# Two norm reductions of a two-layer transformer kernel: one loop over both sources in place of one loop after the other

## The reference

```python
x = L0_attn_x                                   # (8, 2048, 1024) float32
# layer 0
xn = layernorm(x)
s = causal_attention_16_heads(xn, Wq, bq, Wk, bk, Wv, bv, Wo, bo)   # with rope
g = silu(ffn_int8(xn, w_gate, w_up, w_down))
x = x + s * g
# layer 1
xn = layernorm(x)
q = xn @ Wq + bq;  k = xn @ Wk + bk;  v = xn @ Wv + bv
q_sq = sum(q * q, axis=-1)
k_sq = sum(k * k, axis=-1)
dist_sq = q_sq[:, :, None] + k_sq[:, None, :] - 2.0 * (q @ k.T)
scores = exp(-dist_sq)
attn = softmax(scores, axis=-1)
s = (attn @ v) @ Wo + bo
g = silu(mix_of_8_adapters(xn))
x = x + s * g
```

## Time and profile before

| what | us |
|---|---|
| median of 2 runs | 3301.47 |
| the two runs | 3224.66 and 3378.28 |
| profiled execution, its own time | 3231.18 |
| its span on the slowest core (core 6), first to last instruction | 3229.6 |
| spans of the other seven cores | 3203.3 to 3225.4 |
| mean granted TensorE clock of the cores | 0.776 to 0.781 |

### The profile page before, as it was taken

How to read it: one execution, slowest core, us unless ns; L and a number is a source line. 1 busy time by engine, 2 the same in 40 slices (tenths; PEclk the granted TensorE clock), 3 DMA queues, 4 the chain that set the end, 5 groups by cost and what they waited for, 6 DMA issues and landing times.

```text
span 3229.6 us, 39546 instructions; the slowest of 8 cores (3203.3 to 3229.6 us)
## 1 busy us (share of the span) xinstructions
PE 2296.0 (71%) x15153; PEld 1262.9 (39%) x15302; DVE 878.0 (27%) x1693; ACT 861.8 (27%) x1189; POOL 80.4 (2%) x152
## 2 busy tenths in 40 slices
PE   2499989984666646796777777166787564887777
PEld 0244444431333213464664665043575221333333
DVE  1544444442232264433222112500110000122122
ACT  2111111112111145464444444111100223222222
POOL 0000001100000000000000000000000000000000
PEclk9699999997888865656556555588888895988888
DMA  4222222202101020101001000432143102011010
GB/s 120 30 30 30 30 30 34 36 7 52 20 14 19 1 52 1 60 2 60 2 1 60 2 2 11 170 94 72 59 133 97 26 0 52 1 52 39 14 52 27
DMA packets 58442, 128.65 MB, mean 40 GB/s; under 512 B 7561, under 2 KB 15755, under 8 KB 55700
## 3 DMA queue, kind: packets, MB, share of 16 engines
q1 hardware_dynamic: 33364, 90.46, 8.3%
q0 software_dynamic: 24896, 35.66, 7.3%
HBM read 142.88 MB, written 18.88 MB: 50 GB/s over the span
## 4 chain that ended last, share of the span: by engine, by line
PE 57%; ACT 16%; DVE 13%; issue 7%; DMA 5%; DVEq 1%; ACTq 0%; SPq 0%; POOL 0%; PEldq 0%; POOLq 0%
PE PS L886 8%; ACT EB L908 6%; PE PS L720 6%; PE PS L1192 5%; PE PS L592 5%; PE PS L601 5%; PE PS L1335 4%; PE PS L1164 4%; PE PS L1404 4%; PE PS L635 4%; PE PS L1275 2%; DVE PS L891 2%; ACT PRJ L728 2%; DVE ACC L646 1%; PE PS L952 1%
## 5 line engine op out<-in xcount | busy, mean ns | idle before, releaser
L886 PE MATMUL PS<-Q,K 64*128 64x128 bf16 x2176 | 274.1, 304 | 123.8 <-ACT EB L908 118.8
L908 ACT ACTIVATE EB<-PS,negBh 128x1152 bf16<-128x1152 f32 (+7 forms) x128 | 204.1, 1594 | 256.0 <-DVE PS L891 242.0
L886 PEld LDWEIGHTS PS<-Q,K 64*128 64x128 bf16 x2176 | 211.5, 135 | 152.9 <-issue 142.2
L1192 PE MATMUL PS<-XN,W1FULL 128*128 128x512 bf16 x747 | 177.4, 397 | 65.4 <-ACT Q L1207 18.7
L635 PE MATMUL PS<-HT,WDT 128*128 128x512 bf16 x745 | 191.3, 393 | 39.1 <-DVE HT L618 21.9
L720 PE MATMUL PS<-XN,WBLK 128*128 128x512 bf16 x746 | 205.0, 438 | 12.7 <-DVE K L735 5.1
L1164 PE MATMUL PS<-identw,PLAND 128*128 128x128 f32 x1024 | 142.6, 308 | 98.9 <-DMA PLAND<-Wsel 67.6
L891 DVE TENSOR_TENSOR PS<-PS,trinegT 128x128 f32<-128x128 f32 x256 | 76.7, 300 | 439.0 <-PE PS L886 430.7
L1164 PEld LDWEIGHTS PS<-identw,PLAND 128*128 128x128 f32 x1024 | 139.3, 223 | 104.1 <-issue 104.1
L592 PE MATMUL PS<-XN,WGT 128*128 128x512 bf16 x752 | 171.0, 383 | 8.5 <-DVE ACC L646 5.7
L601 PE MATMUL PS<-XN,WUT 128*128 128x512 bf16 x752 | 168.8, 379 | 0.8
(11 more groups left out here) (160 smaller groups left out, 2522.4 us busy)
## 6 DMA issues: line engine op xcount, KB each, us to landing
PLAND<-Wsel SPq DMA_DIRECT2D x64, 512.0 KB, 4.2
XF<-xT SPq DMA_DIRECT2D x1, 8192.0 KB, 35.8
XT<-xT SPq DMA_DIRECT2D x4, 2048.0 KB, 8.5
x1park<-XT SPq DMA_DIRECT2D x32, 256.0 KB
X1CH<-x1park SPq DMA_DIRECT2D x8, 1024.0 KB, 8.5
XT<-x1park SPq DMA_DIRECT2D x4, 2048.0 KB, 8.2
outT<-XT SPq DMA_DIRECT2D x32, 256.0 KB
LAND<-wg POOLq DMA_DIRECT2D x16, 256.0 KB, 4.6
```

The lines of the kernel that those rows point to most:

```text
L886: tS = P.op("tensor", lambda t, h=h, gi=gi, tt=tt, off=off: t.matmul(PS[:, off + tt * 128:off + (tt + 1) * 128], head_k(h, ts(tt, 128)), h ...
L908: s.activation(EB2[:, slot, 0:klen], PS[:, 0:klen], AF.Exp, bias=negBh[:, h:h + 1]), inc=True)
L1192: P.op("tensor", lambda t, fc=fc, j=j, n=n: t.matmul(BK(n), W1FULL[:, j, ts(fc, 128)], src_xn[:, j, ts(n, 512)], start=(j == 0), stop=(j = ...
```

## The change

The two passes over K and Q become one loop over c. In it ScalarE squares the chunk of K into slot c % 2 of `EB2`, VectorE squares the chunk of Q (as Q times Q) into slot c % 2 of `ETB`, seen as 128 x 2 x 2048, and TensorE does four matmuls for K into banks 0 to 3 and then four for Q into banks 4 to 7. Each square waits for the matmuls that read its slot two chunks earlier. The eight row copies on VectorE all stand after the loop.

```diff
-    tM = None
-    for src_, which in ((K, "k"), (Q, "q")):
-        tSq = None
-        for c in range(EC):
-            P.wait("scalar", tM)
-            tSq = P.op("scalar", lambda s, c=c, src_=src_: s.activation(
-                EB2[:, 0, :], src_[:, c, :], AF.Square), inc=True)
-            P.wait("tensor", tSq)
-            for n in range(4):
-                tM = P.op("tensor", lambda t, c=c, n=n: t.matmul(
-                    BK(n), negones[:, :], EB2[:, 0, ts(n, 512)],
-                    start=(c == 0), stop=(c == EC - 1)), inc=(n == 3))
-        P.wait("vector", tM)
-        dst_row = NKSQ_ROW if which == "k" else NQSQ_ROW
-        sclr = 1.0 if which == "k" else 0.25
-        tRw = None
+    tMsl = {0: None, 1: None}
+    tMq = {0: None, 1: None}
+    ETBf = ETB.rearrange("p s a b -> p s (a b)")
+    tMk = tMqq = None
+    for c in range(EC):
+        sl = c % 2
+        P.wait("scalar", tMsl[sl])
+        tks = P.op("scalar", lambda s, c=c, sl=sl: s.activation(
+            EB2[:, sl, :], K[:, c, :], AF.Square), inc=True)
+        P.wait("vector", tMq[sl])
+        tqs = P.op("vector", lambda v, c=c, sl=sl: v.tensor_mul(
+            ETBf[:, sl, :], Q[:, c, :], Q[:, c, :]), inc=True)
+        P.wait("tensor", tks)
         for n in range(4):
-            tRw = P.op("vector", lambda v, n=n, dst_row=dst_row, sclr=sclr:
-                       v.tensor_scalar_mul(dst_row[0:1, ts(n, 512)],
-                                           BK(n)[0:1, :], sclr), inc=(n == 3))
-        P.wait("tensor", tRw)
-        P.wait("scalar", tRw)
+            tMk = P.op("tensor", lambda t, c=c, n=n, sl=sl: t.matmul(
+                BK(n), negones[:, :], EB2[:, sl, ts(n, 512)],
+                start=(c == 0), stop=(c == EC - 1)), inc=(n == 3))
+        tMsl[sl] = tMk
+        P.wait("tensor", tqs)
+        for n in range(4):
+            tMqq = P.op("tensor", lambda t, c=c, n=n, sl=sl: t.matmul(
+                BK(4 + n), negones[:, :], ETBf[:, sl, ts(n, 512)],
+                start=(c == 0), stop=(c == EC - 1)), inc=(n == 3))
+        tMq[sl] = tMqq
+    P.wait("vector", tMk)
+    P.wait("vector", tMqq)
+    tRw = None
+    for n in range(4):
+        tRw = P.op("vector", lambda v, n=n: v.tensor_scalar_mul(
+            NKSQ_ROW[0:1, ts(n, 512)], BK(n)[0:1, :], 1.0), inc=(n == 3))
+    tRw2 = None
+    for n in range(4):
+        tRw2 = P.op("vector", lambda v, n=n: v.tensor_scalar_mul(
+            NQSQ_ROW[0:1, ts(n, 512)], BK(4 + n)[0:1, :], 0.25),
+            inc=(n == 3))
+    P.wait("tensor", tRw2)
+    P.wait("scalar", tRw2)
     P.barrier()
```

## The result

Timed beside the kernel before, the changed kernel has a median of 3221.34 us (17 runs, 3183.85 to 3402.49) against 3261.25 (16 runs, 3224.66 to 3378.28). The ratio is 0.9878, with a 95% interval of 0.9831 to 0.9925: some 1.2% faster, within the 2% that I called the same. Runs in which half of the cores as a whole were slower at a lower clock are left out of this ratio; others with a few cores at a clock near 0.77, the profiled one among them, stay in, and the medians lie so far above the lowest times for both reasons. In a later set of runs the same kernel took 3183.63 to 3186.45 us in four runs beside a median of 3227.76 for the kernel before, ratio 0.9847 (0.9791 to 0.9902).

What follows compares the result with a forecast made beforehand. No engine full; in the norm stage ScalarE and TensorE alternate on one buffer. Q's squares off the chain 15.3 us, TensorE's clock some 11, the rest overlap: 46 us. 3231.2 - 46 = 3185 us, range 3168 to 3262.

Steps and rivals of the forecast that it cites:

- The chain: Norm stage: square and four matmuls alternate strictly on one buffer, 4.01 us a chunk, 70.3 us for the stage.
- ScalarE's squares: New loop: squares 1.86 us apart set the pace; third and fourth start late, the fourth by over 1 us.
- VectorE's product: New loop: each bf16 product of Q taken at 1.23 us; 2.29 as the other end costs 2 us of the gain.
- The clock in the loop: New loop: TensorE begins at the lower level, and the clock rises 3.9 to 5.9 us after the first matmul.
- the clock stays low: Rival, norm loop: clock stays at 0.5, gain 35 us, time 3196; chance 0.17 together with a swinging clock.
- Squares and products in each other's way: Rival, norm loop: ScalarE and VectorE slow each other to 3.1 us a chunk, gain 37, time 3194; chance 0.05.
- The step that failed: Head of last stage: TensorE's pause grows from 3.5 to 5.9 us, costed at nothing, up to 1 us.
- The lottery of the last stage: Last stage: a shifted start deals its granted clocks anew; four query groups some 6 us to either side.
- The level: Whole kernel: 46 us subtracted from the profiled execution's 3231.2 us, giving 3185, not from the timed runs' median.
- the likeliest case: Whole kernel: the forecast of 3185 us with the product at either price, own range 3174 to 3195; chance 0.68.
- A sign of being wrong: Last stage: query groups that take over 130 us each would show the forecast wrong.
- The slower rival: Rival, last stage: a lower clock, from 0.87 to 0.78, uses up the 46 us; chance 0.03.

Runs made afterwards that it cites:

- the two-slot kernel: Kernel before with both slots of EB2 used in turn and nothing else: stage 38.2 to 38.4 us, both stages 533.6 to 544.9 us.
- the kernels with one slot: Changed kernel with one slot for K's squares and one for Q's: stage 32.9 us, both stages 535.2 to 538.1 us.
- with ScalarE alone: Changed kernel with Q's squares moved from VectorE to ScalarE: stage 35.8 to 36.0 us, both stages 536.9 to 538.4 us.
- the kernel with K's norms in the Q projection: Changed kernel without the barrier, K's squares and matmuls moved into the Q projection, Q's squares split between VectorE and ScalarE: ratio to before 0.9808.
- the changed kernel's second profile: The changed kernel run once more, unaltered: stage 23.4 to 23.5 us, last stage 506.5 to 506.9 us, ratio to before 0.9847.
- the run with the fill: Changed kernel plus twelve unread matmuls between K's row copies and the barrier: stage 23.7 to 24.2 us, both stages 523.2 to 524.0 us on five cores.

## Why the prediction was right, and where it wasn't

The forecast was 3185 us, no change clear of 2%. The time of the stage came out by the mechanism that I gave; that the total did so too is in part luck. Point by point:

- **The chain.** That ScalarE and TensorE alternate for want of a second buffer, and that this bounds the stage, is shown by the two-slot kernel: 70.3 to 38.4 us by that alone.
- **ScalarE's squares.** I took 1.86 us from start to start; five in a row took 9.12 us, which is (9.12 - 1.90)/4 = 1.80. The third and fourth squares were held up as laid out (0.30 and 0.56 us, where I had 0.3 and over 1).
- **VectorE's product.** I took 1.23 from a row of another operation, and it measured 1.225; the other end, 2.29, is out. The Trainium skill, "VectorE: DVE Perf Modes", section "The perf-mode tier table", had given 1224 ns, and the trace agrees.
- **The clock in the loop.** I had it rise 3.9 to 5.9 us after the first matmul; it rose after 3.2. The 3.9 was a misreading: 2729.4 is where my window ended, and its mean of 0.59 over 4.0 us puts the rise near 3.3. Together with the squares this makes the stage 23.5 us instead of 24.5, and the gain 46.8 instead of 46. The rival "the clock stays low" had 0.17 and fell: this loop and those of the kernels with one slot and with ScalarE alone kept the higher level once they had it, with pauses of 1.3 us (one slot) and 0.8 us or less (ScalarE alone) between their bursts; the two-slot kernel lost it only in the pause between K and Q. For this loop the rule of the Trainium skill on small pauses between groups ("TensorE: Matmul & The Clock Gate", section "A second HAM failure mode: psum-queue depth-cycling") was not borne out by the trace.
- **Squares and products in each other's way.** They aren't: beside each other a square takes 1.90 us, as before, and a product 1.225, as in the kernel with K's norms in the Q projection, where ScalarE makes no squares beside it (1.23).
- **The step that failed** is "It started that stage at the lower level anyway [...], so I cost this at nothing, with up to 1 us". The pause ahead of the last stage grew from 3.5 to 5.9 us, as I had it, but the clock fell in it and stayed down for 12 us of work: 5.7 us, with the long head on 14 of 16 cores. The term was mis-sized by 5 us. With the pause filled the loss is gone (the last stage takes 499.3 to 500.0 us), so there is none without the pause. But the longer pause isn't the whole cause: with one slot each, with ScalarE alone and on two cores of the changed kernel itself the pause was as long, and the low head took 2.8 to 3.6 us, for which "nothing" would have been right. What made it long here stays open.
- **The lottery of the last stage.** I gave it 6 us to either side. Within the changed kernel's second profile the eight cores agree within 0.4 us, but the two-slot kernel, with the same instructions in that stage, has 495.3 to 506.6 on its eight cores. So the spread is there, and no run says what deals it.
- **The level.** I subtracted from the profiled execution's 3231.2, which is 3.4 us above the later median of the kernel before (its core 6 had a last stage of 504.2 us where the others had 501 to 503). The gain was taken some 4 us too large, 46 against 42. The two errors cancel, and it is by that luck that 3185 was met to the microsecond by 3183.6 to 3186.5. The median beside the first runs of before is 3221, outside the 3174 to 3195 that I gave the likeliest case; only the upper end, which took in a median over runs of unlike clock, covers it.
- **A sign of being wrong** was query groups of over 130 us. One of the four came, the first, with 131.0, and it pointed at the step that failed.
- **The slower rival**, a lower clock in the last stage, had the right place and the right sign, but a size of 5.7 us where 46 were needed.

## What to carry to other kernels

Where two engines alternate on one buffer, count both the wait and what the alternation does to TensorE's clock; the second slot is then the first thing to try, and a second engine for the producer only comes after it. When work ahead of a stage gets denser, look at the pause that it leaves in front of the next one, and measure both stages together: serial copies and a barrier cost the next stage 5.7 us here beyond their own length, in other kernels with the same pause nothing, and no rule in this study tells which. Filling the pause got them back, even with useless matmuls, or better with the next stage's own. A stage whose operands are ready earlier (here K's norms) belongs in the waits of an earlier loop.

## What the runs showed of the hardware that was not expected

**A longer pause can be cheaper, and equal pauses differ.** In the changed kernel a pause of 5.7 to 5.9 us was followed by 12.5 to 12.7 us at 0.50 on 14 cores and by 2.8 to 2.9 on two. In two other kernels pauses of the same length were followed by 3.1 to 3.6 us. With 10.7 to 10.9 us it was 4 on six cores and 8 on two; with 3.5 us it was some 3.3 in the kernel before (a mean of 0.59 over 4.0 us leaves 0.7 for the higher level), and with 3.3 to 3.5 us in the two-slot kernel 8 on six cores. And with the pause filled it was none.

**The same four matmuls a chunk at either level.** In the kernel before the bursts of 1.88 us came every 4.01 us, and the clock stayed at 0.50 for 70 us. In the two-slot kernel eight matmuls ran with next to no pause at first, the clock rose, and then bursts of 1.02 us every 1.80 us kept it at 1.00. What of this brought it up, no run tells.

**A third clock, in pairs of cores.** In the first profile of the changed kernel core 6 lost 36 us between 2100 and 2460 us, in projections that the change doesn't touch. Windows of core 6, within one block of matmuls and over the stretch:

```profile
2152.00:2159.00 7.00, 7.00 (x28) 2.92 (x27) 0.00 (x0) 0.00 (x0) 0.00 (x0) 0.81 0.23 75
2100.00:2460.00 360.00, 277.87 (x1392) 190.40 (x1408) 27.98 (x38) 38.77 (x64) 0.88 (x1) 0.73 0.28 83
```

and of core 2:

```profile
2150.00:2156.00 6.00, 6.00 (x29) 2.70 (x28) 0.00 (x0) 0.00 (x0) 0.00 (x0) 1.00 0.26 87
2100.00:2460.00 360.00, 267.78 (x1663) 195.58 (x1662) 32.77 (x43) 38.77 (x64) 0.88 (x1) 0.88 0.35 102
```

The granted clock is 0.81 within the block, 28 matmuls in 7.00 us against 29 in 6.00, so a value between 0.5 and 1.0 isn't always a mean of the two. The Trainium skill, "TensorE: Matmul & The Clock Gate", Part 1, has a limiter of 13/16 when three cores of a die run dense matmuls; 0.81 agrees with its figure. But it holds the whole die there, and here cores 6 and 7 had it for about 240 us, cores 4 and 5 for 131, in another stage, and cores 0 to 3 not at all; in the run with one slot cores 4 and 5 had it for about 238 us and cores 2 and 3 for 112 to 119, the rest not. In the run with the fill all of cores 4 to 7 had it for some 700 us, but 4 and 5 before 1570 us of their spans and 6 and 7 after 1700. No run of this study chose it or kept it away, so what brings it on stays open. Its size, 36 us on a core, is nearly that of the whole change, and so a page of one execution should be read next to the clocks of all cores.
